# Modulating and normalising h by tokens, one pass ahead, in an adaLN block with mLSTM attention and a mixture of experts

## The chip, the cores and the metric

The kernel runs on one core of a Trainium2 chip, in one launch. The metric is the device time of that launch in microseconds (us). A core has TensorE (PE in the rows; PEld is its weight load), VectorE (DVE), ScalarE (ACT), GpSimd (POOL) and SyncE (SP), each with an instruction queue of its own. They hand work to each other by semaphores.

## The reference

Eight rows of 512 tokens with 128 features go through one block. All is float32.

```python
sa, ca, ga, sb, cb, gb = mod[:, 0..5]           # from silu(c) @ wmod, one vector of 128 per row
ga, gb = sign * maximum(abs, 0.25)
h = layernorm(x) * (1 + ca) + sa
x = x + ga * attn(h)
h = layernorm(x) * (1 + cb) + sb
x = x + gb * moe(h)                              # 8 experts 128 -> 256 -> 128, top 2, dense here
...
def attn(x):                                     # x is the modulated h
    normed = x * rsqrt(mean(x * x) + 1e-6) * norm_w
    q, k, v, zi, zf, o = linear maps of normed   # o through a sigmoid
    scan over t: C, n, m -> h_t = o_t * C_t q_t / max(|n_t . q_t|, 1)
    return x + h_t @ Wout.T
```

The scan is computed as a masked product of scores and weights, all tokens of a row at once. `attn` returns its own input plus the projected result, so `ga * h` is part of the new x.

## The kernel before, in words

A row is a tile of 128 tokens by 4 by 128 features (512 columns). The work is software-pipelined over rows in passes. Pass b, the function `body(b, ...)` that every engine has its own copy of, holds four things: the experts of row b, the end of the attention of row b+1 (`end`), its start for row b+2 (`start`), and the layer norm of row b+3 (`ahead`). Passes run from b = -2 (`first`, no experts) over b = -1 (`opening`) to b = 7. A pass has 16 turns, t = 3 to 18, one for each half expert: in turn t TensorE does the three up matmuls of half expert t and the three down matmuls of half expert t-3 (each operand is split in a high and a low part). Turns 16 to 18 already belong to half experts 0 to 2 of the next row. The order on every engine is written out by hand: it is the program order of `body`, and nothing overtakes in a queue.

For one half expert n the steps are: up on TensorE (L1142 to L1144), `hg` on VectorE (relu and gate, L876), `hg_hi` on ScalarE (high part, L535), `hg_lo` on GpSimd or VectorE (low part, L482 or L889), down on TensorE (L1158, L1159, L1168). GpSimd has the low parts 1 and 8 to 15 of a row (`POOL_STEPS`), so its last one of a pass is number 15 in turn 16, and the next, number 1 of the following row, comes in turn 18.

After turn 18 of pass b ScalarE copies the row's expert sum into `y_sb` with the factor gb (L596), TensorE transposes it (L1107, function `y_transposes`), and VectorE adds it to x. These three stand at the end of `body`, behind turn 18. TensorE's next pass stands behind its transposes.

The start of a row's attention, before: GpSimd normalises by tokens (`norm(0, b+3)`, L445 to L455), a pass ahead. In pass b TensorE transposes (L1009, turn 4), ScalarE modulates on the way out of PSUM with sa and ca as columns (`hT`, L550), squares the same again (`sq`, L553) and makes `h_ga` (hT times ga, L558). TensorE maps to q and k (L1014, turn 6), sums the squares by a matmul with a column of 1/128 (L1019, turn 7, four of one column, eight records), VectorE adds epsilon, GpSimd raises to -1/2 (`rms`, L464), and v, zi, zf and o (L1187, turn 9) are scaled by `rms` as VectorE takes them from PSUM (L815, L821, L830). q and k are not scaled. The denominator is compared with 1/rms in place of 1. At the end of the row's attention TensorE transposes `h_ga` back into the bank of the output product (L988, turn 4) and adds hh @ Wout to it (L999).

The first pass has no experts; TensorE fills its waits with `keep_busy` (L1079). It also makes `wout_ga` (Wout times ga, all rows), for which VectorE writes a diagonal matrix of ga per row (`diag_ga`, L666) and TensorE spreads it over all partitions with a matmul with ones (`row_weights`, L971).

Of the kernel before, what the change touches and what calls it, by code (L numbers as in the profile page):

```python
# [5 lines left out]
def adaln_mlstm_moe_kernel(  # L6
# [77 lines left out]
    with ctx:  # L84
# [61 lines left out]
        rstd = [sb(f"rstd{k}", [P, NT]) for k in range(2)]  # L146
        xn = [sb(f"xn{k}", [P, NT, D]) for k in range(2)]
# [81 lines left out]
        s_b2l = sem("s_b2l")  # L229
        s_whi = sem("s_whi")  # L230
# [117 lines left out]

        def pool_steps(b):
            return LAST_STEPS if b == B - 1 else BEFORE_LAST_STEPS if b == B - 2 else POOL_STEPS  # L350
# [65 lines left out]
        def _(pool):  # L416
# [39 lines left out]

            def body(b, end, start, ahead, live, opening=False):
                m1, m2 = b + 1, b + 2
                for t in range(LAG, N + LAG):
                    if t == 7 and end:  # L460
                        norm(1, m1)
                    if t == 8 and start:
# [3 lines left out]
                        if m2 > 0:  # L466
                            pool.wait_ge(s_v, m2)
# [8 lines left out]
                    if live(t - 1) and (t - 1) % N in pool_steps(b):  # L476

                        k = (t - 1) % 4
                        if t - 1 == 12 and end and start:
                            pool.wait_ge(s_gates, m1 + 1)  # L480
                        pool.wait_ge(s_hghi, b * N + t)
                        g.tensor_tensor(hg_lo[k][:, :], hg[k][:, :], hg_hi[k][:, :].bitcast(fp32), ALU.subtract).then_inc(s_lo_pool, 1)  # L482

# [6 lines left out]
                            pattern=[[1, E], [0, NU], [-1, E]], channel_multiplier=0).then_inc(s_mask0, 1)  # L490
            body(-2, False, True, True, lambda n: False)
# [6 lines left out]
        def _(act):  # L498
# [18 lines left out]

            def body(b, end, start, ahead, live, weights_hi=False, opening=False):
                m1, m2 = b + 1, b + 2
                for t in range(LAG, N + LAG):  # L520
# [15 lines left out]
                    if t == N and (opening or b == B - 2):  # L536
                        act.wait_ge(s_gfirstT, sorted(FIRST_GATE_BANK).index(m1) + 1)
                        a.activation(gate_bc[m1 % 2][:, 0, :], FIRST_GATE_BANK[m1][:, :], ACT.Copy).then_inc(s_gfirst, 1)
                    if weights_hi and t == 7:
# [7 lines left out]
                    if t == 5 and start:  # L547

                        act.wait_ge(s_xT, m2 + 1)
                        a.activation(hT[:, :], bA[:, :], ACT.Identity, bias=mods[:, 0, bass.ds(m2, 1)],  # L550
                                     scale=mods[:, 1, bass.ds(m2, 1)]).then_inc(s_hT, 1)
                    if t == 6 and start:
                        a.activation(sq[:, :], bA[:, :], ACT.Square, bias=mods[:, 0, bass.ds(m2, 1)],  # L553
                                     scale=mods[:, 1, bass.ds(m2, 1)]).then_inc(s_sq, 1)
                    if t == 8 and start:
                        if m2 == 0:
                            act.wait_ge(s_dve0, 3)
# [6 lines left out]
                    if t == 10 and start:  # L564
                        act.wait_ge(s_zo, m2 + 1)
                        a.activation(th[:, :, :], zo[:, :, :], ACT.Tanh, scale=0.5).then_inc(s_th, 1)
                    if t == 10 and start:
# [14 lines left out]
                    if start and t in (14, 15, 16):  # L582
# [4 lines left out]
                        weights(m2, t - 14)  # L587
# [656 lines left out]
```

## Time and profile before

| | us |
|---|---|
| median of 3 timed runs | 331.12 |
| lowest, highest | 327.93, 331.92 |
| profiled execution, its own time | 327.37 |
| its span | 325.6 |
| outside the span | 1.8 |
| TensorE busy | 314.3 (97% of the span) |
| VectorE, GpSimd, ScalarE busy | 264.2, 171.5, 166.0 |

The profiled execution is 0.56 us below the lowest timed run and 3.75 us below their median. Busy times overlap. A PE record's end is modelled, so that neighbouring matmuls overlap in the rows; the distance from start to start tells what one costs in a stream. The granted clock was 1.00 in every stretch read.

### The profile page before, as it was taken

To read this page: it belongs to the slowest core of one execution; us is meant where nothing else is said; L and a number is where in the kernel's file an instruction comes from. 1 tells how busy PE (TensorE), PEld (TensorE's weight loads), DVE (VectorE), ACT (ScalarE), POOL (GpSimd) and SP (SyncE) were. 2 spreads that over 40 slices of the span, in tenths; PEclk is the share of its full clock that TensorE was granted. 3 is DMA by queue.
4 is the path that set the end of the run, shared out by engine and by line. 5 is a ranking of instruction groups with operands and counts; after the bars stand their busy time and mean duration, and the time that the engine had idled before them with its cause. 6 is when DMAs were issued, how large, how long until landed. Compare 5 with 4: busy or idle time off the path is not lost.

```text
span 325.6 us, 5182 instructions
## 1 busy us (share of the span) xinstructions
PE 314.3 (97%) x1775; PEld 257.9 (79%) x1775; DVE 264.2 (81%) x801; ACT 166.0 (51%) x311; POOL 171.5 (53%) x181
## 2 busy tenths in 40 slices
PE   8989989999999999999999999999999999999996
PEld 7778856888887878787788888787888778777995
DVE  5786777998699886998599868987779859987875
ACT  1542525565637645464656473573555564346442
POOL 6450470388626964476538952596506762526440
PEclk9999999999999999999999999999999999999999
DMA  5870002300160007100530017000710034006101
GB/s 135 249 211 0 2 0 75 157 0 0 55 239 3 0 2 260 32 1 0 162 134 1 0 34 259 2 2 1 251 42 1 0 116 179 0 2 209 51 2 32
DMA packets 13456, 23.63 MB, mean 73 GB/s; under 512 B 1763, under 2 KB 8086, under 8 KB 12406
## 3 DMA queue, kind: packets, MB, share of 16 engines
q1 hardware_dynamic: 13202, 23.17, 22.1%
q8 instruction: 14, 0.23, 0.3%
q14 instruction: 12, 0.10, 0.1%
q10 hardware_dynamic: 164, 0.07, 0.1%
q0 software_dynamic: 64, 0.07, 0.1%
HBM read 21.07 MB, written 2.23 MB: 72 GB/s over the span
## 4 chain that ended last, share of the span: by engine, by line
PE 79%; DVE 8%; DMA 6%; ACT 2%; issue 2%; SPq 1%; POOL 1%; DVEq 0%; POOLq 0%
PE bank L1142 9%; PE bank L1144 8%; PE bank L1168 8%; PE bank L1158 8%; PE bank L1143 8%; PE bank L1159 8%; PE bank L1072 6%; DMA gate_bc<-gates_d 3%; PE bank L999 3%; PE bank L1187 2%; PE bank L1014 2%; PE bank L1019 2%; DMA br_bc<-in_L_ffn_br_dram 2%; PE bank L1193 1%; DMA gates_d<-gate_rows 1%
## 5 line engine op out<-in xcount | busy, mean ns | idle before, releaser
L482 POOL TENSOR_TENSOR hg_lo<-hg,hg_hi 128x512 fp32r<-128x512 f32 x65 | 87.4, 1356 | 66.5 <-ACT hg_hi L535 50.6
L876 DVE SCALAR_TENSOR_TENSOR hg<-bank,neg_b,gate_bc 128x512 f32<-128x512 f32 x128 | 94.3, 743 | 25.5 <-DMA gate_bc<-gates_d 13.2
L535 ACT ACTIVATE hg_hi<-hg 128x512 fp32r<-128x512 f32 x128 | 79.8, 629 | 62.2 <-DVE hg L876 60.8
L1142 PE MATMUL bank<-h_hi,w_hi 128*128 128x512 f32 x128 | 58.3, 456 | 1.5 <-ACT gate_rows L581 1.5
L1168 PE MATMUL bank<-hg_lo,w_hi 128*128 128x512 f32 (+1 forms) x144 | 53.2, 369 | 0.0
L1158 PE MATMUL bank<-hg_hi,w_hi 128*128 128x512 f32 (+1 forms) x144 | 53.1, 369 | 0.0
L1159 PE MATMUL bank<-hg_hi,w_lo 128*128 128x512 f32 (+1 forms) x144 | 52.9, 367 | 0.0
L1144 PE MATMUL bank<-h_lo,w_hi 128*128 128x512 f32 x128 | 50.4, 394 | 0.0
L1143 PE MATMUL bank<-h_hi,w_lo 128*128 128x512 f32 x128 | 50.3, 393 | 0.0
L889 DVE TENSOR_TENSOR hg_lo<-hg,hg_hi 128x512 fp32r<-128x512 f32 x63 | 48.0, 761 | 1.1 <-ACT hg_hi L535 0.6
L445 POOL TENSOR_SCALAR var_eps<-mv 128x4 f32<-128x4 f32 x16 | 4.0, 250 | 65.2 <-DVE mv L616 65.2
L1159 PEld LDWEIGHTS bank<-hg_hi,w_lo 128*128 128x128 f32 x144 | 27.1, 188 | 5.5
L1158 PEld LDWEIGHTS bank<-hg_hi,w_hi 128*128 128x128 f32 x144 | 27.0, 188 | 5.3
L1168 PEld LDWEIGHTS bank<-hg_lo,w_hi 128*128 128x128 f32 x144 | 27.0, 188 | 5.2 <-DVE hg_lo L889 0.3
L1142 PEld LDWEIGHTS bank<-h_hi,w_hi 128*128 128x128 f32 x128 | 24.1, 189 | 7.8 <-issue 2.9
L1144 PEld LDWEIGHTS bank<-h_lo,w_hi 128*128 128x128 f32 x128 | 24.0, 188 | 5.5
L1143 PEld LDWEIGHTS bank<-h_hi,w_lo 128*128 128x128 f32 x128 | 24.3, 190 | 3.1 <-issue 1.4
L719 DVE TENSOR_TENSOR ew<-ew,bank 128x512 f32<-128x512 f32 (+3 forms) x32 | 14.8, 482 | 9.0 <-ACT ew L514 8.7
L1072 PEld LDWEIGHTS bank<-vs,ew 128*128 128x128 f32 x160 | 18.5, 192 | 3.0 <-DVE ew L719 2.8
L1072 PE MATMUL bank<-vs,ew 128*128 128x65 f32 x160 | 19.4, 277 | 0.4 <-DVE ew L719 0.2
L452 POOL TENSOR_TENSOR rstd<-var_eps,minus_half 128x4 f32<-128x4 f32 x16 | 19.3, 1205 | 0.0
L455 POOL TENSOR_TENSOR xn<-xn,rstd 128x512 f32<-128x512 f32 x16 | 17.6, 1102 | 2.6 <-POOL rstd L452 0.5
(175 smaller groups left out, 538.9 us busy)
## 6 DMA issues: line engine op xcount, KB each, us to landing
gate_bc<-gates_d SPq DMA_DIRECT2D x8, 1024.0 KB, 7.0
gate_bc<-gates_d SPq DMA_DIRECT2D x8, 512.0 KB, 4.9
gate_bc<-gates_d SPq DMA_DIRECT2D x14, 256.0 KB, 3.7
out_dram<-x_all SPq DMA_DIRECT2D x7, 256.0 KB, 2.3
w_raw<-in_L_ffn_W_dram SPq DMA_DIRECT2D x1, 1024.0 KB, 8.8
x_all<-in_L_attn_x_dram SPq DMA_DIRECT2D x2, 256.0 KB, 4.0
wmod_sb<-in_L_wmod_dram SPq DMA_DIRECT2D x1, 384.0 KB, 4.7
out_dram<-x_all SPq DMA_DIRECT2D x2, 128.0 KB, 1.9
```

The costliest lines, as they stand in the source:

```text
L452: g.tensor_tensor(rstd[k][:, :], var_eps[k][:, :], minus_half[:, :], ALU.pow).then_inc(s_rs[k], 1)
L482: g.tensor_tensor(hg_lo[k][:, :], hg[k][:, :], hg_hi[k][:, :].bitcast(fp32), ALU.subtract).then_inc(s_lo_pool, 1)
L535: a.activation(hg_hi[k][:, :], hg[k][:, :], ACT.Copy).then_inc(s_hghi, 1)
L876: v.scalar_tensor_tensor(hg[k][:, :], up_bank[n % 4][:, :], neg_b1[:, n:n + 1], gate_bc[own % 2][:, n // NU, :], ALU.max, ALU.mult).then_i ...
L889: v.tensor_tensor(hg_lo[k][:, :], hg[k][:, :], hg_hi[k][:, :].bitcast(fp32), ALU.subtract).then_inc(s_lo_dve, 1)
L1072: last = t_.matmul(bA[:, q * NS:(q + 1) * NS], ew[:, o:o + P], vs[:, j, :], start=j == 0, stop=j == q)
L1142: t_.matmul(dst, w_hi, hx, start=True, stop=False)
L1143: t_.matmul(dst, w_lo, hx, start=False, stop=False)
L1144: t_.matmul(dst, w_hi, hl, start=False, stop=True).then_inc(s_up, 1)
L1158: t_.matmul(y[:, c0:c1], w_hi, hg_hi[k][:, c0:c1], start=n == 0, stop=False)
L1159: t_.matmul(y[:, c0:c1], w_lo, hg_hi[k][:, c0:c1], start=False, stop=False)
L1168: last = t_.matmul(y[:, c0:c1], w_hi, hg_lo[k][:, c0:c1], start=False, stop=n == N - 1)
```

## The change

For rows 1 to 7 the tokens' side does what the features' side did. Before the first pass and in it, `diagonals` (GpSimd), `spread` (TensorE, into banks 2 and 3) and `spread_copies` (ScalarE) write 1 + ca and sa of all rows to all partitions (`sc_bc`, `sh_bc`), four rows at a time; `ga_copies` (ScalarE) does it for ga, over `diag_ga`. Then, in pass b for row b+3, behind GpSimd's low part 15 in turn 16 (in the first pass behind `norm(0, 1)`), `modulate` multiplies `xn` by 1 + ca, adds sa, makes ga times that, and adds it to x in SBUF. In turn 17 ScalarE squares `xn` with a sum over the features (`squares`), and GpSimd makes 1/rms of it (`deviation`, two small instructions, in the program behind `modulate`). In turn 18 ScalarE multiplies `xn` by it (`normalise`, four instructions). What TensorE transposes in turn 4 of the next pass is then the finished normed h.

Gone for rows 1 to 7 are L553 and L558 on ScalarE, L1019 and L988 on TensorE, and GpSimd's `rms` and `rms2`; L550 becomes a plain copy; the scaling of v, zi, zf and o by rms becomes an addition of the bias or a copy, in two instructions each in place of four; 1/rms in the denominator becomes 1. v, zi, zf and o move from turn 9 to turn 8 (TensorE waits there for the low parts of k and q, L769, as before), and what follows them by one turn up to the transposed `a_col`. In the first pass TensorE's filler writes to bank 4 and waits for `s_dve0`, and VectorE's `row_weights` waits for `ga_copies`.

```diff
@@ GpSimd
+            def modulate(r):
...
+                g.tensor_tensor(h, h, spread(sc_bc), ALU.mult).then_inc(s_hs, 1)
+                pool.wait_ge(s_hs, r)
+                g.tensor_tensor(h, h, spread(sh_bc), ALU.add).then_inc(s_h, 1)
+                pool.wait_ge(s_h, r)
+                pool.wait_ge(s_gabc, 1)
+                pool.wait_ge(s_ms, 1)
+                g.tensor_tensor(xg3, h, spread(ga_bc), ALU.mult).then_inc(s_xgp, 1)
+                pool.wait_ge(s_xgp, r)
+                g.tensor_tensor(x_row, x_row, xg3, ALU.add).then_inc(s_xg, 1)
+            def deviation(r):
+                pool.wait_ge(s_msq, r)
+                g.tensor_scalar(ms_n[:, :], msq[:, :], 1.0 / D, RMS_EPS, ALU.mult, ALU.add).then_inc(s_msn, 1)
+                pool.wait_ge(s_msn, r)
+                g.tensor_tensor(rms_n[:, :], ms_n[:, :], minus_half[:, :], ALU.pow).then_inc(s_rmsn, 1)
...
                         g.tensor_tensor(hg_lo[k][:, :], hg[k][:, :], hg_hi[k][:, :].bitcast(fp32), ALU.subtract).then_inc(s_lo_pool, 1)
+                    if ahead and t == (9 if first else 16):
+                        modulate(b + 3)
+                    if ahead and t == 17:
+                        deviation(b + 3)
@@ ScalarE
+            def squares(r):
+                act.wait_ge(s_h, r)
...
+                    last = a.activation(y_sb[:, j * P:(j + 1) * P], xn[0][:, j, :], ACT.Square, accum_out=msq[:, j:j + 1])
+            def normalise(r):
+                act.wait_ge(s_rmsn, r)
+                act.wait_ge(s_xgp, r)
+                for j in range(NT):
+                    last = a.activation(xn[0][:, j, :], xn[0][:, j, :], ACT.Copy, scale=rms_n[:, j:j + 1])
+                last.then_inc(s_hn, 1)
...
+                    if ahead and t == 17:
+                        squares(b + 3)
+                    if ahead and t == 18:
+                        normalise(b + 3)
@@ TensorE
-                        for j in range(NT):
+                        for j in range(NT if m1 == 0 else 0):
                             t_.matmul(bC[:, j * P:(j + 1) * P], h_ga[:, j * P:(j + 1) * P], ident[:, :], start=j == 0, stop=False,
...
-                    if t == 7:
+                    if t == 7 and m2 == 0:
                         pe.wait_ge(s_sq, m2 + 1)
...
-                    if t == 9 and start:
+                    if t == (9 if first else 8) and start:
...
+                    if first and t in (7, 16):
+                        spread(0 if t == 7 else 1)
```

ScalarE at the end of a steady pass, before. `hg_hi` with a number is a high part, `ew` the attention weights, `y_sb` the expert sum on its way to the transposes; the names in brackets are semaphores waited for.

```order
L591 ACTIVATE gateT<-gate_rows 72x512 [waits s_grow]
L535 ACTIVATE hg_hi3<-hg3 128x512 [waits s_hg]
L512 ACTIVATE ew<-mb,a_col 128x128 x2
L514 ACTIVATE ew<-bank6,a_col 128x128
L535 ACTIVATE hg_hi0<-hg0 128x512 [waits s_hg]
L535 ACTIVATE hg_hi1<-hg1 128x512 [waits s_hg]
L596 ACTIVATE y_sb<-bank4,mods 128x512 [waits s_dn]
L535 ACTIVATE hg_hi2<-hg2 128x512 [waits s_hg]
L546 ACTIVATE hhT<-bank6 64x512 [waits s_hhT]
```

The same place in the changed kernel:

```order
L698 ACTIVATE gateT<-gate_rows 72x512 [waits s_grow]
L630 ACTIVATE hg_hi3<-hg3 128x512 [waits s_hg]
L576 ACTIVATE ew<-mb,a_col 128x128 x2
L578 ACTIVATE ew<-bank6,a_col 128x128
L630 ACTIVATE hg_hi0<-hg0 128x512 [waits s_hg]
L601 ACTIVATE y_sb,msq<-xn0 128x128 [waits s_h]
L630 ACTIVATE hg_hi1<-hg1 128x512 [waits s_hg]
L609 ACTIVATE xn0<-xn0,rms_n 128x128 [waits s_xgp,s_rmsn]
L609 ACTIVATE xn0<-xn0,rms_n 128x128 x3
L703 ACTIVATE y_sb<-bank4,mods 128x512 [waits s_dn]
L630 ACTIVATE hg_hi2<-hg2 128x512 [waits s_hg]
L647 ACTIVATE hhT<-bank6 64x512 [waits s_hhT]
```

The squares (four, which use `y_sb` as a place to write to) stand between two high parts, and the normalisation, which waits for GpSimd's `s_rmsn`, stands in front of the copy of the expert sum.

GpSimd at the same place, in the changed kernel, from its last two low parts on (before, the next low part, `hg_lo1`, followed `hg_lo3` directly):

```order
L541 TENSOR_TENSOR hg_lo2<-hg2,hg_hi2 128x512 [waits s_hghi]
L541 TENSOR_TENSOR hg_lo3<-hg3,hg_hi3 128x512 [waits s_hghi]
L498 TENSOR_TENSOR xn0<-xn0,sc_bc 128x512 [waits s_xn0,s_sbc]
L500 TENSOR_TENSOR xn0<-xn0,sh_bc 128x512 [waits s_hs]
L504 TENSOR_TENSOR sq<-xn0,diag_ga 128x512 [waits s_ms,s_gabc,s_h]
L506 TENSOR_TENSOR x_all<-x_all,sq 128x512 [waits s_xgp]
L511 TENSOR_SCALAR ms_n<-msq 128x4 [waits s_msq]
L513 TENSOR_TENSOR rms_n<-ms_n,minus_half 128x4 [waits s_msn]
```

Six instructions are new between low part 15 and low part 1 of the next row.

TensorE at the end of the first pass, in the changed kernel. `L1108` and `L1109` are the last scores, `L1218` the spread of rows 4 to 7, `L1224` filler, `L1209` the product of weights and v; before, filler and that product followed the scores directly.

```order
L1108 MATMUL bank7<-qq,kk 128x256 [waits s_P]
L1109 MATMUL bank7<-qz,kk 128x256
L1218 MATMUL bank2<-gate_bc1,ones 128x512 [waits s_sbc,s_dg]
L1218 MATMUL bank3<-gate_bc1,ones 128x512
L1224 MATMUL bank4<-ones,ident 128x128 x4
L1209 MATMUL bank5<-vs,ew 128x65 [waits s_vcol,s_P]
```

The spread waits for GpSimd's second pair of diagonals (`s_dg`), which stand behind `norm(0, 1)` and `modulate(1)` on GpSimd.

## Rows read from the trace of the kernel before

**Rows 1.** Busy time by stretch: two steady passes, from turn 4 to turn 4

```profile
96.70:132.40 35.70, 35.24 (x197) 29.01 (x196) 29.99 (x94) 19.70 (x38) 22.01 (x20) 1.00 0.20 68
203.50:239.10 35.60, 35.26 (x196) 29.00 (x195) 30.06 (x94) 19.70 (x38) 22.00 (x20) 1.00 0.21 68
```

**Rows 2.** What TensorE waited for, from 93 to 270 us (total, times, longest)

```profile
PE bank L1142 <- ACT gate_rows L581: 1.3, 5, 0.3
```

**Rows 3.** The chain that ended last, in order of time (start, us, what)

```profile
132.45 0.44 PE bank L988 x4
...
140.08 0.79 PE bank L1019 x8
```

**Rows 4.** Timeline at the end of pass b = 1 (start, us, engine, line, operation)

```profile
123.28 1.30 POOL L482 TENSOR_TENSOR hg_lo<-hg,hg_hi 128x512 fp32r<-128x512 f32 x1 [0.39 <-ACT hg_hi L535]
...
127.18 0.63 ACT L535 ACTIVATE hg_hi<-hg 128x512 fp32r<-128x512 f32 x1 [0.56 <-DVE hg L876]
127.71 0.67 ACT L596 ACTIVATE y_sb<-bank,mods 128x512 f32<-128x512 f32 x1
127.88 1.84 POOL L482 TENSOR_TENSOR hg_lo<-hg,hg_hi 128x512 fp32r<-128x512 f32 x1 [3.31 <-ACT hg_hi L535]
127.89 0.69 DVE L889 TENSOR_TENSOR hg_lo<-hg,hg_hi 128x512 fp32r<-128x512 f32 x1
...
128.82 0.60 PE L1107 MATMUL bank<-ident,y_sb 128*128 128x128 f32 x4
...
131.76 0.41 DVE L780 TENSOR_TENSOR hh<-uh,rden 128x256 f32<-128x256 f32 x1
```

**Rows 5.** The same view at the end of pass b = 0

```profile
88.02 1.29 POOL L482 TENSOR_TENSOR hg_lo<-hg,hg_hi 128x512 fp32r<-128x512 f32 x1 [0.39 <-ACT hg_hi L535]
...
93.13 0.60 PE L1107 MATMUL bank<-ident,y_sb 128*128 128x128 f32 x4
```

**Rows 6.** Durations of single lines (ns: least, median, most; first and last start)

```profile
L455 POOL TENSOR_TENSOR xn<-xn,rstd x16: 1039/1041/1218, 9.0 to 282.9; 128x512 f32<-128x512 f32 x16
L482 POOL TENSOR_TENSOR hg_lo<-hg,hg_hi x65: 1262/1293/1851, 58.0 to 316.1; 128x512 fp32r<-128x512 f32 x65
L445 POOL TENSOR_SCALAR var_eps<-mv x16: 227/228/575, 6.6 to 280.0; 128x4 f32<-128x4 f32 x16
L452 POOL TENSOR_TENSOR rstd<-var_eps,minus_half x16: 1031/1040/1490, 7.8 to 281.2; 128x4 f32<-128x4 f32 x16
L512 ACT ACTIVATE ew<-mb,a_col x32: 389/396/403, 24.6 to 265.8; 128x128 f32<-128x128 f32 x32
```

**Rows 7.** Timeline of the first pass, ScalarE's weights, two in one row

```profile
26.07 0.69 ACT L512 ACTIVATE ew<-mb,a_col 128x128 f32<-128x128 f32 x2
```

**Rows 8.** Timeline of a steady pass, turns 7 and 8

```profile
139.92 0.95 PE L1019 MATMUL bank<-mean_col,sq 128*128 128x1 f32 x8
140.73 0.48 PE L1142 MATMUL bank<-h_hi,w_hi 128*128 128x512 f32 x1
140.96 0.68 DVE L769 TENSOR_TENSOR qq<-bank,qq 64x512 fp32r<-64x512 f32 x1
...
142.20 0.39 PE L1142 MATMUL bank<-h_hi,w_hi 128*128 128x512 f32 x1
```

**Rows 9.** Timeline of the first pass and into the opening

```profile
18.96 1.04 POOL L452 TENSOR_TENSOR rstd<-var_eps,minus_half 128x4 f32<-128x4 f32 x1
...
20.14 1.08 POOL L455 TENSOR_TENSOR xn<-xn,rstd 128x512 f32<-128x512 f32 x1
...
26.64 1.05 PE L1079 MATMUL bank<-ones,ident 128*128 128x128 f32 x8
27.53 2.44 PE L1072 MATMUL bank<-vs,ew 128*128 128x65 f32 x20
...
39.30 1.96 PE L1084 MATMUL bank<-w_raw,ident 128*128 128x512 f32 x4
...
42.45 0.86 DVE L815 SCALAR_TENSOR_TENSOR zo<-bank,rms,bo_bc 128x64 f32<-128x64 f32 x4 [1.39 <-PE bank L1187]
```

More of the change, by code:

```diff
@@ L461, in body @@
                         norm(1, m1)
-                    if t == 8 and start:
+                    if first and t == 10:
+                        diagonals(1)
+                    if t == 8 and first:
                         pool.wait_ge(s_mse, m2 + 1)
@@ L538, in body @@
                         a.activation(gate_bc[m1 % 2][:, 0, :], FIRST_GATE_BANK[m1][:, :], ACT.Copy).then_inc(s_gfirst, 1)
+                    if first and t == 7:
+                        spread_copies(0)
+                    if first and t == 11:
+                        ga_copies()
+                    if first and t == 17:
+                        spread_copies(1)
                     if weights_hi and t == 7:
@@ L563, in body @@
                                      scale=mods[:, 4, bass.ds(m1, 1)]).then_inc(s_h2, 1)
-                    if t == 10 and start:
+                    if t == (10 if first else 9) and start:
                         act.wait_ge(s_zo, m2 + 1)
                         a.activation(th[:, :, :], zo[:, :, :], ACT.Tanh, scale=0.5).then_inc(s_th, 1)
-                    if t == 10 and start:
+                    if t == 10 and first:
                         act.wait_ge(s_rms, m2 + 1)
@@ L1027, in chain @@
                 if start:
[L1028 removed]
+                    if t == (11 if m2 == 0 else 10):
                         pe.wait_ge(s_v, m2 + 1)
@@ L1073, in chain, with spread, keep_busy @@
                         last.then_inc(s_pv, 1)
-            def keep_busy(n):
+            def spread(n):
+                pe.wait_ge(s_dg, n + 1)
+                if n:
+                    pe.wait_ge(s_sbc, n)
+                for k in range(2):
+                    last = t_.matmul(bank[2 + k][:, :], ones[:, :], diag(n, k), start=True, stop=True)
+                last.then_inc(s_spr, 1)
+            def keep_busy(n, dst):
                 for _ in range(n):
-                    t_.matmul(bank[3][:, 0:P], ident[:, :], ones[:, :], start=True, stop=True)
+                    t_.matmul(dst[:, 0:P], ident[:, :], ones[:, :], start=True, stop=True)
             def keep_busy_wide(n):
@@ L1113, in body @@
                         first_gates(B - 1)
+                    if first and t == LAG + 1:
+                        pe.wait_ge(s_dve0, 1)
+                    if opening and t == LAG + 1:
+                        pe.wait_ge(s_sbc, 2)
                     if first and t > LAG or opening and LAG < t < 8:
-                        keep_busy(2)
+                        keep_busy(2, bank[4] if first else bank[3])
                     if opening and t == 8:
```

126 lines of the change are left out of this document (102 added, 24 removed).

## The prediction

> **What bounds the kernel now.** I read the busy times by stretch first. In a steady pass of 35.6 to 35.7 us TensorE is busy for 35.2, and no other engine for more than 30.1 [rows 1]. The waits say the same from the other side: between 93 and 270 us TensorE itself waits in one place only, 1.3 us in five passes [rows 2]. So in the middle of the kernel an instruction taken from TensorE is worth its place in the stream, and a wait put on TensorE costs its full length. The chain of waits gives those places: the four h_ga transposes take 0.44 us and the eight records of the sum of squares 0.79 us of a pass [rows 3].
>
> Then I looked at the end of a pass in the timeline, because there the change puts new work into two queues [rows 4]. GpSimd ends low part 15 at 123.28 + 1.30 = 124.58 and is free until 127.88. ScalarE copies the expert sum into y_sb at 127.71. TensorE's transposes of it start at 128.82, right behind the product of weights and v, without a wait. So from the end of low part 15 to these transposes there are 128.82 - 124.58 = 4.24 us. In pass b = 0 it is 93.13 - 89.31 = 3.82 [rows 5]; the other three passes that have both work `ahead` and a y_sb (b = 2 to 4) lie between these two. I take 4.1 as their mean. That is all the time the new chain has before TensorE notices it.
>
> **The change part by part.**
>
> *The new chain at the end of passes 0 to 4.* In the new order ScalarE has the four normalising instructions in front of y_sb, and they wait for `rms_n`, the last of six instructions that GpSimd starts when low part 15 is done. TensorE's transposes wait for y_sb, and the whole next pass stands behind them in TensorE's queue. So TensorE has to wait for this sum, counted from the end of low part 15:
>
> - `modulate`: four instructions of 128x512. No such form is in the trace. The nearest rows are L455 with one full operand, 1.04, and L482 with two, 1.29 [rows 6]; I take 1.17 each, 4.7, bounds 4.2 and 5.2. Three of them wait for the one before: L455 starts 0.14 after L452's end (18.96 + 1.04 to 20.14) [rows 9], so 0.4 more.
> - VectorE beside it: low part 1 took 1.84 where VectorE's low part started 0.01 us later, in place of 1.30 [rows 4]. Two VectorE instructions of that kind fall in this stretch. I take 0.5 for one, bounds 0 and 1.1.
> - `deviation`: 0.23 as L445, 0.14, and 1.04 as L452, 1.4 together; 1.9 if the power meets VectorE (1.49 is the most in L452) [rows 6]. The squares on ScalarE start after the second of the four instructions and need four times about 0.3 to 0.4, less than the other two take, so they are hidden; only if one took over 0.7 would they show.
> - `normalise`: four of 128x128. One such ScalarE instruction takes 0.40 [rows 6], two in a row 0.69 [rows 7], so four take 0.40 + 3 x 0.29 = 1.3, at most 1.6. Then y_sb, 0.67 of which 0.1 overlaps (127.18 + 0.63 to 127.71), and three handovers of about 0.1, 0.9 together [rows 4].
>
> The sum is 4.7 + 0.4 + 0.5 + 1.4 + 1.3 + 0.9 = 9.2 us, bounds 8.1 and 11.1. Less the 4.1 that are there, TensorE stands still for 5.0 us (4.0 to 7.0) at the end of each of five passes: **+25 us** (20 to 35). The Trainium skill (SBUF — State Buffer, section "SBUF: two separate sides") says that GpSimd and VectorE take turns on a shared pair of ports, the loser blocked for the winner's whole instruction. By that rule the second item would be up to twice 0.69, 1.4 in place of my 0.5, and the sum 4 to 5 us higher over five passes; the row's 0.54 for one overlap agrees with a block that GpSimd shares only in part.
>
> What waits with it is covered: high part 2 comes behind y_sb, but TensorE is behind its transposes by then too; low part 1 comes 1.3 after `deviation`, before y_sb is done; hh, which VectorE makes behind adding the transposed rows, ends 3.35 us after the transposes start today (131.76 + 0.41) [rows 4], and TensorE reaches it, without h_ga, at about the same time.
>
> *What TensorE loses, as a gain.* The h_ga transposes go in passes 0 to 6: 7 x 0.44 = 3.1 at most. hh is ready 3.35 after the transposes of y_sb and the h_ga transposes fill TensorE just up to then, so part of the 0.44 turns into a wait for hh; I take 0.3 each, 2.1. The sum of squares goes in passes 0 to 5: 6 x 0.79 = 4.7 at most. But v, zi, zf and o follow one turn earlier, behind the low parts of k and q. Turn 9 starts at 142.20; without L1019 turn 8 would end at 141.41, and L769 ends at 141.64 [rows 8]. So a wait of 0.23 and a handover comes in its place; I keep 0.4 of the 0.79, 2.4 over six passes. Together **-4.5 us**, bounds -7.8 (all of it) and -2.
>
> *The first pass.* Row 1's `norm` ends on GpSimd at 20.14 + 1.08 = 21.2 [rows 9], now some 0.5 later, because TensorE spreads rows 0 to 3 before it makes v, zi, zf and o. Behind it stand `modulate(1)`, 5.1, and the second pair of diagonals, 2 x 1.17 = 2.3: 29.1. TensorE waits for them in front of the product of weights and v: the spread is two matmuls of 512 columns, four records, 1.9 as L1084 x4; then the filler, 0.9 from start to start of 26.64 and 27.53 [rows 9]. The product starts at 31.9 in place of 27.53: **+4.4 us**. If the GpSimd instructions take 1.04 and nothing else is late it is 3.1; if they take 1.3 and the third waits 1 us for `ga_copies` behind ScalarE's two large conversions, 6.2. Everything behind is serial through TensorE, so it counts in full. Row 1's normalised h follows about 4 us behind the spread and TensorE has the b2 products in between, so that wait is hidden.
>
> *The opening (b = -1).* The 0.79 goes here too, and VectorE's path from L815 on (0.86 for four) [rows 9] becomes two instructions. Against that, ScalarE's high part 2 waits for the squares and the normalisation of row 2, since low part and deviation come only after high part 0. I set both at 1 to 1.5 and take **0**, bounds -1.5 and +1.5.
>
> ScalarE's own balance (two instructions of 512 columns go, eight of 128 come) and VectorE's shorter instructions lie beside TensorE and count nothing.
>
> *Sum.* 25 - 4.5 + 4.4 + 0 = 24.9 on the profiled execution's own 327.37: 352.3. That execution lies at the lower end of the runs shown (327.93 to 331.92, median 331.12); I add 2 us, about half its distance to the median, for a median of **354 us**. Bounds: 327.4 + 20 - 7.8 + 3.1 - 1.5 = 341; 327.4 + 35 - 2 + 6.2 + 1.5 = 368, and 372 at the median's whole distance.
>
> **The rivals.**
>
> *Not slower: the chain is covered.* If GpSimd were done with its six instructions when TensorE comes to the transposes, the change would show only its gain. It decides at 4.1 us from low part 15 to the transposes. Of the 9.2 ScalarE's part alone is 2.2, so GpSimd would have 1.9 us for six instructions of which each large one has never taken less than 1.04. For it speaks that TensorE's saving is real and that GpSimd and ScalarE each have over 13 us free in a pass [rows 1]; against it the order, in which nothing passes y_sb. The time would be 327.4 - 7.8 + 4.4 + 2 = 326, and 322 if the first pass were covered too. Chance 5%.
>
> *The clock falls in the stalls.* The granted clock is 1.00 (2.4 GHz) in every stretch, but TensorE never stands still there [rows 1, 2]; now it would for 5 us, five times. A turn of six matmuls takes about 1.4 us (140.73 to 142.20) [rows 8]; each turn at half the clock costs as much again. One turn after each stall gives 5 x 1.4 = 7 us, 361; two give 368. No row here shows such a gap, so I cannot exclude it. The Trainium skill (TensorE: Matmul & The Clock Gate, section "HAM oscillation — how this bites in real kernels") says that a TensorE which waits between bursts falls to the half clock and starts each burst there. Chance 27%.
>
> *A shorter stall.* If GpSimd's four instructions take 1.04 and never meet VectorE, and if the whole 7.8 of TensorE's gain is kept, it is 341 to 346. Chance 10%.
>
> **How the numbers follow.** The forecast as summed, 354, has 58%, with 347 to 360 as its own range; the clock on top 27%; the short stall 10%; covered 5%. The range 342 to 371 leaves out the covered case and the ends of the others. A measurement of this kernel can tell about 2%, here 6.6 us: faster than 324.5 is half of the covered case, 2%; within 2% the rest of it and the least of the short stall, 5%; slower 93%.
>
> **What would show it.** In the changed profile TensorE waits for ScalarE's y_sb at the transposes, five times, 4 to 7 us each, and ScalarE waits for GpSimd's rms_n just before. The six GpSimd instructions fill the time from low part 15 on; L988's and L1019's counterparts have 4 and 8 records in place of 32 and 64; TensorE waits for the diagonals at about 28 us. The clock's row in the busy times by stretch decides the second rival. The prediction is wrong if TensorE waits under 2 us at these transposes, or if the wait stands in another place, as at v, zi, zf and o or at low part 1.

## The result, and the profile after

The changed kernel takes 368.63 us (367.89 to 369.56, 4 runs) against 329.86 us (327.93 to 331.92, 4 runs) before: the ratio is 1.123, with a 95% interval of 1.118 to 1.128. It is slower, by more than the 354 us of the forecast and inside the range that was given with it. The profiled execution took 368.55 us with a span of 366.8, against 327.37 and 325.6. Line numbers below are those of the kernel that a row is from; an insertion shifts them by a few from one experiment to the next.

The page's row of TensorE's clock was full throughout before; now it has dips in the first pass and one after each of five passes:

```profile
PEclk9898999999978999699978999699987999999999
```

The waits of the changed kernel (total, times, longest) answer to [rows 2], where TensorE waited 1.3 us in all between 93 and 270 us:

```profile
PE bank L1252 <- ACT y_sb L703: 25.9, 6, 5.2
ACT xn L609 <- POOL rms_n L513: 17.0, 7, 2.9
...
PE bank L1337 <- DVE qq L876: 2.9, 7, 1.4
...
PE bank L1125 <- DVE hh L887: 1.2, 1, 1.2
```

The first line is the forecast's stall, TensorE's transposes of y_sb waiting for ScalarE. The second is its cause one engine up, ScalarE's normalise waiting for GpSimd's rms_n. How they hang together is seen in the timeline at the end of pass b = 0, the place of [rows 5]:

```profile
96.47 1.30 POOL L541 TENSOR_TENSOR hg_lo<-hg,hg_hi 128x512 fp32r<-128x512 f32 x1 [0.39 <-ACT hg_hi L630]
97.72 1.30 POOL L498 TENSOR_TENSOR xn<-xn,sc_bc 128x512 f32<-128x512 f32 x1
99.10 1.28 POOL L500 TENSOR_TENSOR xn<-xn,sh_bc 128x512 f32<-128x512 f32 x1
99.56 2.45 PE L1209 MATMUL bank<-vs,ew 128*128 128x65 f32 x20
...
100.45 1.60 POOL L504 TENSOR_TENSOR sq<-xn,diag_ga 128x512 f32<-128x512 f32 x1
...
100.95 1.65 DVE L1017 TENSOR_TENSOR hg_lo<-hg,hg_hi 128x512 fp32r<-128x512 f32 x1
...
102.13 1.59 POOL L506 TENSOR_TENSOR x_all<-x_all,sq 128x512 f32<-128x512 f32 x1
103.80 0.20 POOL L511 TENSOR_SCALAR ms_n<-msq 128x4 f32<-128x4 f32 x1
104.08 1.02 POOL L513 TENSOR_TENSOR rms_n<-ms_n,minus_half 128x4 f32<-128x4 f32 x1
...
105.13 1.28 ACT L609 ACTIVATE xn<-xn,rms_n 128x128 f32<-128x128 f32 x4 [2.93 <-POOL rms_n L513]
106.32 0.67 ACT L703 ACTIVATE y_sb<-bank,mods 128x512 f32<-128x512 f32 x1
107.04 1.12 PE L1252 MATMUL bank<-ident,y_sb 128*128 128x128 f32 x4 [5.03 <-ACT y_sb L703]
```

Read it from the bottom up. The transposes wait 5.03 us for y_sb; y_sb stands behind normalise; normalise waits for the last of six GpSimd instructions that run with gaps of under 0.1 us from the end of low part 15 (96.47 + 1.30 = 97.77). TensorE was through with the product of weights and v at 99.56 + 2.45 = 102.01. The transposes themselves take 1.12 us in place of the 0.60 of [rows 5], which points to the clock. Busy times by stretch (length, then busy time of PE, PEld, DVE, ACT and POOL, then the granted clock, DMA share and GB/s) answer to [rows 1]:

```profile
113.10:155.00 41.90, 36.19 (x183) 28.95 (x182) 31.25 (x88) 20.45 (x47) 26.77 (x24) 0.92 0.16 57
...
102.00:107.00 5.00, 0.01 (x1) 0.00 (x0) 1.73 (x5) 2.07 (x7) 4.09 (x5) 0.88 0.08 33
107.00:110.00 3.00, 2.96 (x9) 2.57 (x10) 1.22 (x2) 0.50 (x1) 0.00 (x0) 0.50 0.05 14
110.00:112.00 2.00, 2.00 (x6) 1.53 (x5) 1.22 (x4) 0.63 (x1) 0.00 (x0) 0.50 0.39 110
112.00:114.00 2.00, 2.00 (x13) 1.65 (x13) 1.46 (x6) 0.26 (x1) 0.00 (x0) 0.84 0.00 0
114.00:116.00 2.00, 2.00 (x12) 1.46 (x11) 2.00 (x8) 1.68 (x4) 0.96 (x2) 1.00 0.00 0
```

This steady pass (b = 1) is 41.9 us long where it was 35.6 to 35.7; the five passes with a stall take 41.5 to 42.8. TensorE does nothing from 102 to 107 and then works for over five microseconds at a clock of 0.50, the lower level of 1.2 GHz: 9 matmul records in three microseconds, where 114 to 116 has 12 in two.

One more view is worth having for everything that follows: where the four transposes of hh (turn 4) start in each pass. Their distances cut the span into parts that can be compared between kernels. All are from the timelines of one profiled execution each, in us; that of e3 is the slower of its two runs (343.64 us, the other took 339.89):

| part of the span | before | after | e2 | e3 | e5 | e9 |
|---|---|---|---|---|---|---|
| start to turn 4 of the opening | 32.4 | 39.1 | 39.2 | 39.1 | 38.3 | 34.5 |
| opening (b = -1) | 29.3 | 31.3 | 31.3 | 30.0 | 30.0 | 27.5 |
| passes 0 to 4 | 177.7 | 210.9 | 200.7 | 187.0 | 181.3 | 176.8 |
| pass 5 | 35.4 | 34.7 | 34.7 | 34.8 | 34.7 | 34.1 |
| the rest | 50.8 | 50.9 | 50.9 | 50.9 | 50.9 | 50.9 |

Of the 41.2 us, 33.2 came in passes 0 to 4, 6.6 in the first pass and 2.0 in the opening. The first row needs care: it moves by itself between kernels with the same code there (41.7 us in e1's profiled run), because the first loads do not land at the same time and the clock can fall there too. In e1 TensorE waits 0.63 us for wmod_sb against 0.21 in the change, and the granted clock is 0.50 from 12 to 16 us where the change has 0.59 and 1.00.

### The profile page after: what moved, and what is told of

Its sections match the earlier page's. It is cut to its first block, busy times and chain, and to the rows that moved or that the text cites. A ratio compares the mean times of both kernels' runs of the same rounds, so it can differ in the third digit from the quotient of the medians.

```text
span 366.8 us, 5095 instructions
## 1 busy us (share of the span) xinstructions
PE 325.1 (89%) x1699; PEld 260.2 (71%) x1699; DVE 273.3 (75%) x760; ACT 173.8 (47%) x380; POOL 210.2 (57%) x213
## 4 chain that ended last, share of the span: by engine, by line
PE 55%; DVE 17%; POOL 14%; ACT 8%; issue 3%; DMA 1%; SPq 1%; POOLq 0%; DVEq 0%
PE bank L1291 6%; PE bank L1293 5%; PE bank L1292 5%; PE bank L1307 5%; PE bank L1308 5%; PE bank L1317 5%; DVE hg L1004 4%; POOL hg_lo L541 4%; DVE hg_lo L1017 3%; PE bank L1337 2%; PE bank L1224 2%; POOL sq L504 2%; POOL x_all L506 2%; DVE stats L717 2%; ACT xn L609 2%
## 5 line engine op out<-in xcount | busy, mean ns | idle before, releaser
L541 POOL TENSOR_TENSOR hg_lo<-hg,hg_hi 128x512 fp32r<-128x512 f32 x65 | 84.0, 1304 | 43.9 <-ACT hg_hi L630 28.0
L1291 PE MATMUL bank<-h_hi,w_hi 128*128 128x512 f32 x128 | 60.9, 476 | 1.5 <-ACT gate_rows L684 1.5
L1017 DVE TENSOR_TENSOR hg_lo<-hg,hg_hi 128x512 fp32r<-128x512 f32 x63 | 53.4, 848 | 2.3 <-ACT hg_hi L630 1.7
L1307 PE MATMUL bank<-hg_hi,w_hi 128*128 128x512 f32 (+1 forms) x144 | 54.9, 381 | 0.0
L1308 PE MATMUL bank<-hg_hi,w_lo 128*128 128x512 f32 (+1 forms) x144 | 54.6, 379 | 0.0
L1293 PE MATMUL bank<-h_lo,w_hi 128*128 128x512 f32 x128 | 52.0, 406 | 0.0
L1292 PE MATMUL bank<-h_hi,w_lo 128*128 128x512 f32 x128 | 52.0, 406 | 0.0
L1317 PEld LDWEIGHTS bank<-hg_lo,w_hi 128*128 128x128 f32 x144 | 27.7, 192 | 5.9 <-POOL hg_lo L541 0.3
L1252 PE MATMUL bank<-ident,y_sb 128*128 128x128 f32 x32 | 7.6, 377 | 25.9 <-ACT y_sb L703 25.9
L1252 PEld LDWEIGHTS bank<-ident,y_sb 128*128 128x128 f32 x32 | 4.9, 190 | 26.9 <-ACT y_sb L703 26.9
L834 DVE TENSOR_TENSOR x_all<-x_all,bank 128x512 f32<-128x512 f32 (+1 forms) x9 | 5.6, 627 | 23.8 <-PE bank L1252 23.8
L1209 PEld LDWEIGHTS bank<-vs,ew 128*128 128x128 f32 x160 | 18.5, 192 | 2.2 <-DVE ew L826 2.2
```

What stands on the lines that cost most here:

```text
L1017: v.tensor_tensor(hg_lo[k][:, :], hg[k][:, :], hg_hi[k][:, :].bitcast(fp32), ALU.subtract).then_inc(s_lo_dve, 1)
L1209: last = t_.matmul(bA[:, q * NS:(q + 1) * NS], ew[:, o:o + P], vs[:, j, :], start=j == 0, stop=j == q)
L1291: t_.matmul(dst, w_hi, hx, start=True, stop=False)
L1292: t_.matmul(dst, w_lo, hx, start=False, stop=False)
L1293: t_.matmul(dst, w_hi, hl, start=False, stop=True).then_inc(s_up, 1)
L1307: t_.matmul(y[:, c0:c1], w_hi, hg_hi[k][:, c0:c1], start=n == 0, stop=False)
```

## The experiments

**e1: normalise behind y_sb.** ScalarE copies y_sb first and normalises afterwards; the squares' unused outputs get a buffer of their own, because y_sb's is then still being read.

```diff
-                    if ahead and t == 18:
+                    if ahead and t == 18 and not live(N - 1):
                         normalise(b + 3)
...
                         a.activation(y_sb[:, c0:c1], y[:, c0:c1], ACT.Copy, ...
+                    if ahead:
+                        normalise(b + 3)
```

> Only the place of the normalisation on ScalarE is changed: in passes 0 to 4 it stands behind the copy of the expert sum into y_sb (the squares write to a buffer of their own, so that this is possible). Theory (TensorE waits because y_sb stands behind rms_n in ScalarE's queue): the five waits of TensorE at the transposes, 25.7 us together, go; what comes next is high part 2, now behind the normalisation, and through it hh, and GpSimd's low part 1: by the changed kernel's own times 1 to 3 us of TensorE's wait per pass in one or two pieces. With shorter gaps the clock stays at 1.00 there, or falls for less. Time 340 to 348. Rival (GpSimd's chain itself is late for TensorE, through low part 1, and y_sb only happens to be the last): the wait moves to another line and stays at about 5 us a pass, the clock falls as before, time 364 or more.

Measured: 348.83 us (347.82 to 349.84), ratio 1.061 (1.052 to 1.069); 20 us below the change, and 0.8 above the upper end of what was expected. The order of two things in ScalarE's queue is about half of the loss of 39 us, with the half clock that hung on it. The wait did not go altogether, though, and it moved. The timeline of e1 at the same place, and its busy times two microseconds on, show

```profile
104.78 0.67 ACT L702 ACTIVATE y_sb<-bank,mods 128x512 f32<-128x512 f32 x1
...
105.50 0.83 PE L1253 MATMUL bank<-ident,y_sb 128*128 128x128 f32 x4 [1.04 <-ACT y_sb L702]
...
107.80 1.28 ACT L608 ACTIVATE xn<-xn,rms_n 128x128 f32<-128x128 f32 x4 [2.35 <-POOL rms_n L514]
```

```profile
106.00:108.00 2.00, 2.00 (x7) 1.61 (x6) 1.41 (x4) 0.20 (x1) 1.83 (x4) 0.50 0.00 0
```

y_sb is still 1 us late, now behind the four squares, and even that wait of 1.04 us is followed by a stretch at half the clock; normalise then holds ScalarE at 107.80 when it should make the next high part. The clock falls like this in the first two of the five passes only. They are no longer than the other three, 37.8 to 38.0 us each, in which TensorE waits 1.2 us for hh instead: where another engine sets the pace, the half clock cost nothing that shows. Passes 0 to 4 take 189.2 us in its trace, 2.3 each more than before.

**e2: the stall kept, TensorE kept at work in it.** Five matmuls of 512 columns whose result nobody reads stand ahead of the transposes in passes 0 to 4.

```diff
+                if b <= B - 4:
+                    for _ in range(5):
+                        t_.matmul(bC[:, :], ident[:, :], w1_raw[:, 0:2, :]..., start=True, stop=True)
                 for k, (y, c0, c1) in enumerate(y_banks(b)):
```

> The changed kernel with five filler matmuls of 512 columns (0.91 us each by the opening's filler) on TensorE in front of the transposes of passes 0 to 4; nothing waits for them and the bank they write is overwritten by the transposes. Theory (after the stalls TensorE works at half the clock for 3 to 5.5 us, and this costs about half of that each time, 11 us in all): granted clock 1.00 behind the stalls, hh transposes about 36.5 + 3.5 us apart in place of 41.5 to 42.8, time 356 to 360. Rival (the half clock is hidden, because other engines set the pace after a stall): clock 1.00 and the time within 3 us of 368.6.

Measured: 357.88 us (357.36 to 358.39), ratio 1.088 (1.083 to 1.094). The wait for y_sb is the same, only filled, and yet the kernel is 10.8 us faster. The timeline of e2, and its busy times where the change had half the clock:

```profile
101.90 4.51 PE L1250 MATMUL bank<-w_raw,ident 128*128 128x512 f32 x10
107.18 0.66 PE L1255 MATMUL bank<-ident,y_sb 128*128 128x128 f32 x4 [0.77 <-ACT y_sb L703]
...
110.68 0.60 PE L1125 MATMUL bank<-ident,hh 128*64 128x128 f32 x4
```

```profile
106.00:108.00 2.00, 1.23 (x7) 0.78 (x7) 0.12 (x1) 1.65 (x4) 0.48 (x1) 1.00 0.00 0
```

From the transposes of y_sb to those of hh it is 3.50 us here and 113.11 - 107.04 = 6.07 in the change; over the five passes 17.5 against 27.7. So the clock is a cost of its own: 10.2 us over five passes, and the passes as a whole differ by the same amount (210.9 - 200.7). Beside it stand the five waits of the change, 5.03 + 5.19 + 5.10 + 5.20 + 5.16 = 25.7. Taken from start to start, which leaves the modelled ends out, the way from the product of weights and v to the transposes of y_sb grew by 26.5 in five passes, from 11.3 to 37.8. What remains of the 33.2 us is TensorE's saving: 10.2 + 26.5 - 33.2 = 3.5 in five passes, 0.7 each. Pass 5, which has no stall, is 0.7 shorter as well (35.4 to 34.7).

**e3: GpSimd's and ScalarE's parts split.** GpSimd only scales and shifts before low part 1 and adds h times the gate to x behind `deviation`; ScalarE squares behind y_sb and normalises in turn 3 of the next pass, into a buffer of its own. `modulate` now only scales and shifts, and `residual` does the rest of it.

```diff
                     if ahead and t == (9 if first else 16):
                         modulate(b + 3)
-                    if ahead and t == 17:
+                        if first:
+                            residual(b + 3)
+                    if ahead and t == (17 if first else 18):
                         deviation(b + 3)
+                        if not first:
+                            residual(b + 3)
...
+                    if t == 3 and 0 <= b <= B - 3:
+                        normalise(b + 2)
```

> Passes -1 to 4 reordered: GpSimd does the first two instructions of modulate behind low part 15, then low part 1, then the deviation, then ga times h and the addition to x; ScalarE copies y_sb first, then squares, and normalises in turn 3 of the next pass into a buffer of its own, which TensorE transposes. The first pass is as in the changed kernel. Theory (only the queue order at the end of the pass costs, 25.7 us of waiting and some 11 us of half clock): no wait of over 0.5 us at the transposes, clock 1.00 there, passes of 35 us from hh to hh (0.5 to 1 us less than before the change), time 329 to 334, the remainder above the old time standing before the first experts. Rival (GpSimd's 5 us more per pass hinder VectorE and its own low parts wherever they stand): passes of 37 us or more.

Measured: 341.76 us (339.89 to 343.64), ratio 1.039 (1.025 to 1.054): 27 us off, and still 8 above what was expected. No wait for y_sb is left. In its place TensorE waits for VectorE's hh in turn 4, 7.3 us in five passes, with half the clock behind two of the three waits of 1.9 us. The passes of 36.9 to 38.3 us are the rival's (37 or more), not the theory's 35. The timeline of e3 at the end of pass b = 1, and the durations of that one line (ns: least, median, most), name the reason:

```profile
139.59 1.29 POOL L509 TENSOR_TENSOR sq<-xn,diag_ga 128x512 f32<-128x512 f32 x1
...
140.97 1.63 POOL L511 TENSOR_TENSOR x_all<-x_all,sq 128x512 f32<-128x512 f32 x1
141.40 1.48 DVE L898 TENSOR_TENSOR hh<-uh,rden 128x256 f32<-128x256 f32 x1
143.03 0.65 PE L1136 MATMUL bank<-ident,hh 128*64 128x128 f32 x4 [1.90 <-DVE hh L898]
```

```profile
L898 DVE TENSOR_TENSOR hh<-uh,rden x8: 424/1482/1523, 37.6 to 290.3; 128x256 f32<-128x256 f32 x8
```

hh is an instruction with both operands in SBUF. It took 0.41 us in [rows 4]; beside GpSimd's addition to x it takes 1.48 and ends 0.28 us after that addition does. The Trainium skill (SBUF — State Buffer, section "SBUF: two separate sides") has VectorE and GpSimd share a pair of ports there, the loser blocked for the winner's whole instruction. These rows agree for VectorE, which began second and had 0.28 of its 0.41 us left when the addition ended. They do not for the winner: the addition took 1.63 us, where the least of its line is 1.27.

**e4: the first pass alone.** The change's passes as they are; in the first pass GpSimd makes both pairs of diagonals at once, the second spread stands in turn 11, its copies in turn 13, and TensorE's filler no longer waits for VectorE's small instructions up to turn 7.

```diff
-                    if first and t == 10:
-                        diagonals(1)
...
             diagonals(0)
+            diagonals(1)
...
-                    if first and t in (7, 16):
+                    if first and t in (7, 11):
                         spread(0 if t == 7 else 1)
```

> The changed kernel with another first pass: GpSimd makes both pairs of diagonals at once, TensorE spreads rows 4 to 7 in turn 11 in place of 16, ScalarE copies them in turn 13, and TensorE's filler writes to its old bank up to turn 7, so that it does not wait for s_dve0. Theory (the 6.7 us by which the first product of weights and v is late come from the wait for the diagonals, the spread itself, the wait for s_dve0 and two falls of the clock): the product starts at 29 to 31 in place of 34.2, time 363 to 366. Rival (VectorE's low parts of the weights, lengthened beside GpSimd, set the first pass): the product starts at 33 or later and the time stays within 1.5 us of 368.6.

Measured: 365.29 us (364.41 to 366.16), ratio 1.111 (1.103 to 1.119). As expected, 3.3 us off. The product of weights and v starts at 31.55 in place of 34.23, half a microsecond later than expected; it was 27.53 in [rows 9].

**e5: the residual behind hh.** One wait more in e3.

```diff
                         deviation(b + 3)
                         if not first:
+                            pool.wait_ge(s_hh, b + 3)
                             residual(b + 3)
```

> The split kernel (e3_split) with one wait more: GpSimd's two residual operations stand behind VectorE's product of turn 3 (the attention head's rows times the reciprocal denominators). Theory: what was left in e3_split is that product, two operands in SBUF, which took 1.48 to 1.52 us beside GpSimd's residual against 0.41 us in the kernel before, so that TensorE waited for it 7.3 us in five passes, with the clock at half behind the longer waits. With the residual behind it the product takes about 0.4 us, TensorE's waits for it come to 2 to 3 us, and the time to 332 to 336 us. Rival: VectorE is late there for another reason (its queue is longer); then the waits stay at 6 to 8 us and the time at 340 to 343 us.

Measured: 337.82 us (336.95 to 338.32), ratio 1.030 (1.026 to 1.035): 4 us below e3 by the medians (e3's two runs lie 3.8 apart, so that the size is not firm) and 2 above the theory's upper end. Timeline of e5, and the durations of hh's line:

```profile
103.92 0.41 DVE L899 TENSOR_TENSOR hh<-uh,rden 128x256 f32<-128x256 f32 x1
...
104.41 1.29 POOL L509 TENSOR_TENSOR sq<-xn,diag_ga 128x512 f32<-128x512 f32 x1 [0.94 <-DVE hh L899]
104.64 0.60 PE L1137 MATMUL bank<-ident,hh 128*64 128x128 f32 x4
```

```profile
L899 DVE TENSOR_TENSOR hh<-uh,rden x8: 407/416/425, 36.8 to 283.6; 128x256 f32<-128x256 f32 x8
```

Every hh is back at 0.41, and the waits for it fell from 7.3 to 1.6 us: the collision was the cause. It is the place of GpSimd's work that hindered VectorE, not its amount, which is the same in both. Delaying GpSimd made the kernel faster. But the time won made TensorE early somewhere else: its wait for VectorE's qq, ahead of v, zi, zf and o, rose from 2.9 us in the change to 6.5.

**e6: VectorE adds the experts' rows behind hh.** `out_rows` of the pass before moves behind hh in turn 3, and TensorE waits for it ahead of turn 5's matmul into the same bank.

```diff
-                if live(N - 1) and b != B - 2:
+                if b == B - 1:
                     out_rows(b)
...
                             v.tensor_tensor(hh[:, :, :], ...).then_inc(s_hh, 1)
+                    if t == LAG + 1 and b > 0:
+                        out_rows(b - 1)
```

> e5_late, and VectorE adds the experts' output to its rows behind that product, not ahead of it (0.68 us earlier for the product). Theory: the wait for the product goes altogether in all five passes, 330 to 334 us. Rival: the bank that the sum reads comes free later, TensorE waits in turn 5 for it, and the time is that of e5_late or above.

Measured: 337.18 us (336.39 to 337.74), ratio 1.028 (1.024 to 1.033). TensorE's waits for hh halve to 0.8 us and three for the bank appear, 0.6 in all: the rival, near enough. It cannot be told from e5.

**e7: e6 with e4's first pass**, and without the two filler groups beside the spreads.

```diff
-                    if first and t > LAG or opening and LAG < t < 8:
+                    if first and t > LAG and t not in (7, 11) or opening and LAG < t < 8:
```

> e6_rows, with the first pass of e4_start (both pairs of diagonals at once, the second spread in turn 11) and without the filler matmuls beside the two spreads. Theory: the first pass's cost is separate from the passes' and adds: e4_start took 3.3 us off, the fillers are 4 groups of 0.45 us or less, so 3 to 5 us below e6_rows, 326 to 331 us. Rival: TensorE's clock falls in the gaps that the fillers covered; then 0 to 2 us below e6_rows.

Measured: 332.38 us (331.94 to 332.93), ratio 1.013 (1.008 to 1.017): 4.8 us below e6. The first pass's cost adds to that of the passes, as expected, though both e6 and e7 lie above the ranges given for their times, by 3.2 and 1.4 us.

**e8: the opening.** GpSimd's last normalising instruction and its modulation wait for the gates there, and v, zi, zf and o go back to turn 9 in this one pass.

```diff
                     if ahead and t == (9 if first else 16):
+                        if opening:
+                            pool.wait_ge(s_gates, 1)
                         modulate(b + 3)
```

> e7_start, and in the opening pass GpSimd's last operation of the normalisation and the modulation stand behind VectorE's gates, and v, the gates' inputs and o are projected in turn 9 as before the change. Theory: TensorE waits there for the gates 1.5 us and for the low part of q 1.4 us, both because VectorE's small instructions stand beside GpSimd's long ones or one turn too early: 1 to 3 us below e7_start, 324 to 329 us. Rival: the modulation of row 2 then ends later and its normalised rows are late at the first steady pass: 0 to 2 us above e7_start.

Measured: 330.70 us (330.19 to 333.10, 9 runs), ratio 1.008 (1.005 to 1.011); 1.7 below e7, as the theory's difference has it, though the time is 1.7 above the range given for it. TensorE's wait for the gates in the opening, 1.5 us in e7, is gone, and that for qq there fell from 1.4 to 0.5. The opening takes 28.5 us in e8's trace and 30.0 in e7's. (The profiled execution of e8 is the slowest of its nine, 333.10 us.)

**e9: v, zi, zf and o in turn 9 of every pass**, and what follows from them a turn later, where the kernel before had it.

```diff
-                    if t == (9 if first or opening else 8) and start:
+                    if t == 9 and start:
                         wait_apart(pe, s_kqlo, b + 3)
```

> e8_open, and in every pass v, the gates' inputs and o are projected in turn 9, and what follows from them one turn later, as in the kernel before (the change had drawn them a turn ahead). Theory: with the stall gone TensorE now reaches that projection before VectorE has the low part of q ready, 0.8 us in each steady pass of e8_open (5.0 us in seven passes); a turn later the wait goes: 3 to 4 us below e8_open, 326 to 328 us, not distinguishable from the kernel before or a little faster. Rival: the attention's chain behind it (decay, mask, exponentials) ends the pass, and the turn lost there comes back as a wait for the weighted scores: 330 us or above.

Measured: 326.63 us (325.57 to 329.42 in ten runs, 332.32 in an eleventh), ratio 0.9955 (0.9928 to 0.9983): 4.1 below e8, and the only one of these kernels below the kernel before. The half per cent is less than the 2% from which a kernel counts as faster here, so that it is as fast as before. One line of e8's timeline and two of e9's waits show what went:

```profile
112.01 1.16 PE L1355 MATMUL bank<-wvzo,hT 128*128 128x130 f32 x8 [0.81 <-DVE qq L891]
```

```profile
PE bank L1335 <- DVE hg_lo L1033: 2.0, 5, 0.5
...
PE bank L1355 <- DVE qq L891: 0.5, 1, 0.5
```

The seven waits for qq, 5.0 us in e8, are one of 0.5, and only 2.0 us of a new one, for VectorE's low parts, came for them. The busy times of a steady pass of e9, to be laid beside [rows 1]:

```profile
97.70:132.90 35.20, 34.33 (x184) 27.57 (x183) 29.30 (x88) 20.33 (x48) 27.20 (x25) 1.00 0.20 68
```

This pass (b = 1) is 35.2 us where it was 35.7, and TensorE's busy time fell by 0.9. The others gained less: passes 0 to 4 together are 0.9 us shorter than before, and pass 5 is 1.3 shorter. With 1.8 in the opening that is 4.0 us, of which the first pass takes 2.1 back.

## Why the prediction was right, and where it fell short

*The stall* was right in place, cause and size. Its six y_sb waits come to 25.9 us, five of them 5.0 to 5.2 each, for a forecast of 25 us in five passes; from start to start it is 26.5. The chain from low part 15 to the transposes is 9.27 us (97.77 to 107.04) for 9.2 summed, and the time there was 4.24 for 4.1. Inside, two terms were off in opposite directions. The durations of GpSimd's new lines (ns: least, median, most) are

```profile
L498 POOL TENSOR_TENSOR xn<-xn,sc_bc x7: 1262/1297/1303, 22.8 to 266.6; 128x512 f32<-128x512 f32 x7
L500 POOL TENSOR_TENSOR xn<-xn,sh_bc x7: 1272/1277/1602, 24.1 to 268.0; 128x512 f32<-128x512 f32 x7
L504 POOL TENSOR_TENSOR sq<-xn,diag_ga x7: 1267/1599/1601, 25.8 to 269.3; 128x512 f32<-128x512 f32 x7
L506 POOL TENSOR_TENSOR x_all<-x_all,sq x7: 1263/1592/1596, 27.5 to 271.0; 128x512 f32<-128x512 f32 x7
```

so the upper bound of 1.3 was the right value for a scale that is spread over tokens, not the 1.17 taken between two rows; and meeting VectorE cost the third and fourth 0.3 each, 0.6 together for 0.5. The handovers were dearer in the sum than in the trace (0.14 between two GpSimd instructions against 0.08). In this chain it was VectorE that lost more: its low part beside the third and fourth took 1.65 us (L1017 above), where the median of its line is 0.68. The prediction weighed a rule of the Trainium skill there (SBUF — State Buffer, section "SBUF: two separate sides"), that the loser is blocked for the winner's whole instruction, and by it the sum would have been 4 to 5 us higher; the chain did not lose that. e1 confirms the cause: with the order on ScalarE turned round, and a buffer for the squares that this needs, 20 us go.

*The clock* is where the number failed. It stood as a rival of 27%, at 361 us for one turn at half clock behind each stall and 368 for two, and the forecast's own sum set it at nothing. The step that failed is the step from "the clock is 1.00 in every stretch" to the likeliest case, since in no such stretch did TensorE stand still. e2 measures it: 10.2 us over five passes, 2.05 a pass, between the two prices of the rival. That the time measured falls on the rival's 368 is luck: the clock alone would have given 364, and the rest came from other terms, below. What the Trainium skill (TensorE: Matmul & The Clock Gate, section "HAM oscillation — how this bites in real kernels") says of bursts that begin at half the clock is what the change's five passes show, with 0.50 for 3 to 6 us behind each wait.

*TensorE's gain* was right in size: 3.5 us in five passes (e2) and 0.7 in pass 5, less 0.1 in the rest of the span, 4.1 in all, for 4.5 with bounds of 2 and 7.8. The wait that was to come at v, zi, zf and o is there, 0.2 to 0.3 us in each of these passes; it was forecast at 0.23 us and a handover. With the stall gone it grows to 0.8 us a pass (e8), which the prediction did not see: its estimate held only behind a TensorE that was late anyway.

*The first pass* cost 6.6 us for 4.4, and the mechanism was another. These rows of the change's timeline answer to [rows 9], and below them stand its busy times by stretch:

```profile
10.61 1.20 PE L1224 MATMUL bank<-ones,ident 128*128 128x128 f32 x4 [1.01 <-DVE mag_g L759]
...
16.04 1.96 PE L1218 MATMUL bank<-gate_bc,ones 128*128 128x512 f32 x4
...
26.64 0.22 PE L1184 MATMUL bank<-ident,m_chunk 4*128 4x4 f32 x1 [1.20 <-DVE m_chunk L844]
...
28.68 2.48 POOL L484 TENSOR_TENSOR gate_bc<-ident,mods 128x512 f32<-128x512 f32 x2
31.62 1.88 PE L1218 MATMUL bank<-gate_bc,ones 128*128 128x512 f32 x4
34.23 2.34 PE L1209 MATMUL bank<-vs,ew 128*128 128x65 f32 x20
```

```profile
10.00:12.00 2.00, 1.39 (x6) 1.42 (x7) 1.90 (x12) 0.00 (x0) 1.85 (x4) 0.56 0.73 238
12.00:14.00 2.00, 2.00 (x13) 2.00 (x12) 1.50 (x9) 1.24 (x2) 2.00 (x3) 0.59 1.09 361
...
27.00:31.00 4.00, 4.00 (x21) 3.96 (x22) 3.88 (x8) 1.68 (x5) 3.92 (x4) 0.57 0.00 0
```

The diagonals do end at 31.16, later than the 29.1 of the sum, but TensorE reaches the spread at 31.62 without a wait for them. It had lost its time before: a wait of 1.01 us for VectorE at 10.61 that was not there before, about half the clock from 10 to 14 us around it, the first spread (1.96 us, which the sum counted only as 0.5 on GpSimd), and half clock again at 27 to 31 us behind three more waits (0.68, 0.46 and 1.20 us). So the term "TensorE waits for the diagonals" was wrong, and "plus the spread" was one spread short. e4, which takes away the early wait and the late diagonals, brings back 3.3 us (2.6 by the first row of the table, where it has 36.5).

*The opening* was set at 0 with 1.5 either way and cost 2.0:

```profile
56.81 1.26 POOL L498 TENSOR_TENSOR xn<-xn,sc_bc 128x512 f32<-128x512 f32 x1
56.85 1.34 DVE L914 TENSOR_TENSOR gates<-gate_a,gate_b 128x96 f32<-128x96 f32 x1
58.24 0.63 PE L1328 MATMUL bank<-ident,gates 128*72 128x128 f32 x4 [1.48 <-DVE gates L914]
```

TensorE waits 1.48 us for the gates, of which VectorE's instruction of 96 elements per partition, begun 0.04 us after GpSimd's, takes 1.34; then 1.23 for hh at the next turn 4. The prediction spoke of high part 2 here, and had no term for small VectorE instructions beside GpSimd's long ones.

Put together on the profiled execution, from 352.3 to 368.55: 10.2 for the clock, 2.2 for the first pass, 2.0 for the opening, 1.5 for the stall and 0.4 for the smaller gain are 16.3 for the 16.25 us. The parts are cut from the same traces, so that they have to add up and the sum proves nothing. The split between first pass and the rest carries the scatter of the first row of the table; that between stall and clock rests on e2.

What stays open: why e5 to e7 end 1 to 3 us above what was summed for them. Their waits for qq, 5.8 to 6.5 us against 2.9 in the change, are of that size, but no run took those away without moving the rest of the attention a turn as well.

## What to carry to other kernels

Before work is moved into a gap on another engine, look at what stands behind it in that engine's queue and who waits for that: GpSimd and ScalarE had over 13 us free in a pass, and about half of the loss came from four instructions put in front of one copy (e1). A wait on a TensorE that sets the pace is to be priced with the clock, here 2 us on top of 5. And an instruction of the critical chain that VectorE takes from SBUF is to be kept clear of GpSimd's long ones in time, by a wait on GpSimd if need be: that wait took TensorE's waits for hh from 7.3 to 1.6 us and made e5 about 4 us faster than e3.

## What the runs showed that was not expected

- The clock fell behind short waits as well, where TensorE had worked until then, but not behind all. In e1 it was at 0.50 behind waits of 1.04 and 0.96 us at the transposes, and at 1.00 behind 0.91, 0.69 and 0.37. In e3 it fell behind two of three waits of 1.9 us. In e2, with filler ahead of the transposes, it stayed at 1.00 behind all five, 0.91 us at most.
- VectorE's small instructions are not safe beside GpSimd: 128x96 took 1.34 us, 128x256 1.48, against 0.26 and 0.41 in the kernel before. In these two pairs the length of GpSimd's instruction counts, not the size of VectorE's.
- Which of a pair that meets pays more is not always the same. In the stall's chain GpSimd's 1.28 us became 1.60 and VectorE's low part lost about 1.0. In [rows 4], where the two began 0.01 us apart, GpSimd's low part took 1.84 in place of 1.30 and VectorE's stayed at 0.69.
